# A graph network kernel on one core: VectorE's messages of the closing item, and TensorE's sums of them, stand one slot earlier in the step

## The chip, the cores and the metric

The kernel runs on one core of a Trainium2 chip. Times are microseconds on the device, from the start to the end of the program. The metric is the median over several executions. One further execution was recorded by the profiler, and all rows below come from it.

## The reference, cut to what matters

A graph has 6,250 nodes and 206,250 edges, sorted by destination. Three attention layers run over it, then a dense block with batch normalization. The change touches only the layers:

```python
xl = (x @ Wl + bl).reshape(n, heads, outc)
e_feat = leaky_relu(xl[src] + (x @ Wr + br).reshape(n, heads, outc)[dst], 0.2)
logits = einsum('ehc,hc->eh', e_feat, att)
m = segment_max(logits, dst)
a = exp(logits - m[dst])
a = a / segment_sum(a, dst)[dst]
out = segment_sum(xl[src] * a[:, :, None], dst)
```

`xl[src] * a` is what the kernel calls the messages, 128 numbers for each edge, and the outer `segment_sum` is what it calls the sums. Layer 1 also adds up 96 edge attributes for each node.

## The kernel before, in words

Edges are cut into chunks of 26 tiles of 128 edges. A chunk, together with a window of 128 destination nodes, is an *item*; each layer has 62 of them here. The 26 tiles of an item fall into 7 groups (`GROUPS`, `NG` = 7): six of four tiles and a last one of two.

All engines run the same software pipeline (`pipeline`), written out by hand in each engine's program. One *step* works on two items at once. It **opens** item k+1: its `xl` rows are gathered by GpSimd, TensorE expands the destination's transform (`expand`, line 763), VectorE adds the two into `z` (line 1186), takes the leaky ReLU with the attention vector (`am`, line 1193), adds up the heads (line 1202, in the last layer 1205) and adds the linear part (line 1216). In the same step it **closes** item k: VectorE finds the segment maxima by scans (lines 1243 to 1275), ScalarE takes the exponential (line 953), VectorE makes the messages (`message(g)`, line 1285), and TensorE sums them into one PSUM bank (`sums(g)`, line 791: 26 products, each of which stands as two passes in the trace, so 52 passes a step). When the last product is done, VectorE merges the item into the state of its nodes, beginning with `new_max` (line 1294), and only behind that does it come to the first group of the next step.

A step of each engine has 7 *slots*, g = 0 to 6. In slot g VectorE handles group g of the opening item. Which messages of the closing item it makes at the end of a slot is read from the table `SUMS_AT`, and TensorE reads its sums from the same table with one slot of delay:

```python
# VectorE, at the end of slot g
if closes and g == NG - 1: new_max()
if closes:
    for m in SUMS_AT.get(g, ()): message(m)
# TensorE, slot g
if opens and g + 2 < NG: expand(opens, g + 2)
if closes and stage == 0 and g in EA_CUTS: attribute_sums(EA_CUTS[g])
if closes:
    for m in SUMS_AT.get(g - 1, ()): sums(m)
```

`attribute_sums` (line 783) exists in layer 1 alone, in TensorE's slots 3, 4 and 5. GpSimd issues 26 gathers an item (line 706). Ahead of the gathers of group g it waits for `message(g)` of the item two before, whose buffer they fill, and for `z` of the group two before: so the gathers of the next item's group 0 wait for `z` of group 5, those of its group 1 wait for `z` of group 6, and those of its group 2 wait for the next step's first `z`. ScalarE makes the one-hot matrices `S` and `ST` for TensorE. SyncE loads the items; in layer 1 the loads of the edge attributes follow `attribute_sums`.

Of the kernel before, what the change touches and what calls it, by code (L numbers as in the profile page):

```python
# [46 lines left out]
NO_NODE = 100000  # L47
GROUPS = [range(a, min(a + 4, TILES)) for a in range(0, TILES, 4)]
NG = len(GROUPS)
SUMS_AT = {2: (0,), 3: (1, 2), 4: (3, 4), 5: (5, 6)}  # L50
EA_CUTS = {3: range(0, 9), 4: range(9, 18), 5: range(18, TILES)}
LH = TILES * HEADS
SQ = 32
# [49 lines left out]
def gnn_program(nc, x, x_t, edges_t, dst_rows, dst, dst_short, edge_attr, node_id, Wl, bl, Wr, br, att, c, g, be,  # L103
                u, W1, b1, gamma, beta, W2, b2, out):
    ctx = ExitStack()
    with ctx:
# [604 lines left out]
        def _(pe):  # L711
# [24 lines left out]
            for stage in range(LAYERS):  # L736

                def pe_step(opens, closes, begins, turned):
# [47 lines left out]
                    def sums(g):  # L786
                        q, v, use = closes
                        pe.wait_ge(onehot_done[g], v * 2)
                        pe.wait_ge(msg_done[g], v + 2)
                        for t in GROUPS[g]:  # L790
                            last = pe.matmul(agg_ps, S[:, q, t, :], msg[:, t, :], start=t == 0 and stage > 0, stop=t == TILES - 1)  # L791
                        if g == NG - 1:
                            last.then_inc(agg_done, 1)
# [3 lines left out]
                    for g in range(NG):  # L797
# [10 lines left out]
                        if closes:  # L808
                            for m in SUMS_AT.get(g - 1, ()):
                                sums(m)  # L810
# [230 lines left out]
        def _(dve):  # L1041
# [130 lines left out]
            def edge_step(stage, opens, closes, begins, turned):  # L1172
# [107 lines left out]
                def message(g):  # L1280
                    q, v, use = closes
                    a, n = GROUPS[g][0], len(GROUPS[g])
                    if g == 0:
                        dve.wait_ge(alpha_done, v)
                    dve.tensor_tensor(out=msg[:, a:a + n, 0:F].rearrange("p t (h f) -> p t h f", h=HEADS),  # L1285
                                      in0=xl_g[:, q, a:a + n, 0:F].rearrange("p t (h f) -> p t h f", h=HEADS),
                                      in1=msg[:, a:a + n, M_ALPHA:M_ONE].unsqueeze(3).to_broadcast([P, n, HEADS, F // HEADS]),
                                      op=ALU.mult).then_inc(msg_done[g], 1)
# [74 lines left out]
                for g in range(NG):  # L1363
# [24 lines left out]
                    if closes:  # L1388
                        for m in SUMS_AT.get(g, ()):
                            message(m)  # L1390
# [152 lines left out]
```

## Time and profile before

| | |
|---|---|
| median of 3 runs | 8529.99 us (8517.47 to 8535.05) |
| profiled execution, own time | 8491.84 us |
| its span on the core | 8489.9 us |
| mean granted TensorE clock | 0.679 |
| busy: TensorE, VectorE, ScalarE, GpSimd | 57%, 62%, 51%, 56% |

No engine is busy for much over half of the span, so the time is made of waits between engines, and one has to read steps, not shares. In a timeline row the columns are start, length, engine, line, operation, tiles and count; what stands in brackets is how long the engine sat idle before the row, and what ended that. "DVE" is VectorE, "PE" TensorE, "POOL" GpSimd. "issue" and "remote" mean that no other instruction of the profile explains the end of the idle time.

### The profile page before, as it was taken

What the parts mean: (1) busy time and instruction counts of PE and PEld (TensorE: products, weight loads), DVE (VectorE), ACT (ScalarE), POOL (GpSimd) and SP (SyncE); (2) the same over time, 40 slices, a digit from 0 to 9 for tenths busy, and PEclk for the clock granted to TensorE, in tenths of its full rate; (3) what the DMA queues carried; (4) which work ended last, traced back from release to release, by engine and by line L of the source; (5) the groups of instructions that cost most, each with busy time, mean ns of one, the idle gap of its engine ahead of it and who ended that gap; (6) DMA issues with size and microseconds to landing.
All of it is one profiled execution on the core that took longest, in us unless ns stands there. A gap on an engine that the chain in (4) does not pass through costs nothing.

```text
span 8489.9 us, 109176 instructions
## 1 busy us (share of the span) xinstructions
PE 4879.8 (57%) x24176; PEld 4286.7 (50%) x24176; DVE 5222.4 (62%) x16308; ACT 4307.0 (51%) x10681; POOL 4740.8 (56%) x4843
## 2 busy tenths in 40 slices
PE   4666666666666655555555555545555555544446
PEld 3565656565656544444444444444444444444444
DVE  5555565656565656766666667655555555555556
ACT  3444444444454545555555555545555555555546
POOL 3555555555555545666666666656666666666640
PEclk7666666666666666766767767666666666666666
DMA  5333333333333322322322323222222222222221
GB/s 147 94 100 91 96 97 97 97 96 97 96 98 95 98 67 74 79 76 76 77 75 77 82 77 78 76 66 72 77 71 71 72 72 72 76 73 72 72 61 50
DMA packets 460163, 697.83 MB, mean 82 GB/s; under 512 B 140781, under 2 KB 330019, under 8 KB 460101
## 3 DMA queue, kind: packets, MB, share of 16 engines
q0 software_dynamic: 154752, 327.15, 16.9%
q1 hardware_dynamic: 305349, 370.00, 14.2%
q8 instruction: 21, 0.34, 0.0%
q14 instruction: 41, 0.34, 0.0%
HBM read 638.95 MB, written 57.76 MB: 82 GB/s over the span
## 4 chain that ended last, share of the span: by engine, by line
PE 33%; issue 27%; DVE 22%; another core or an unknown queue 7%; ACT 6%; POOL 3%; DMA 2%; SPq 0%; DVEq 0%; ACTq 0%; POOLq 0%
PE PS L791 14%; PE PS L763 10%; PE PS L783 6%; DVE z L1186 3%; POOL xl_g L706 3%; DVE am L1193 3%; DVE msg L1285 2%; ACT distT L931 2%; ACT ST L936 2%; DVE relu_logit L1202 1%; ACT dist L906 1%; PE PS L749 1%; DMA xl_g<-xl_tab,edges 1%; DVE relu_logit L1205 1%
## 5 line engine op out<-in xcount | busy, mean ns | idle before, releaser
L706 POOL DMA_INDIRECT xl_g<-xl_tab,edges x4836 | 4740.0, 980 | 3485.8 <-DVE z L1186 1689.1
L763 PE MATMUL PS<-xr_w,ST 128*128 128x132 f32 x9672 | 2054.2, 373 | 2160.7 <-issue 1278.8
L763 PEld LDWEIGHTS PS<-xr_w,ST 128*128 128x128 f32 x9672 | 1778.9, 269 | 2455.4 <-issue 1735.2
L791 PE MATMUL PS<-msg,S 128*128 128x137 f32 x9672 | 1829.7, 352 | 936.8 <-issue 648.7
L791 PEld LDWEIGHTS PS<-msg,S 128*128 128x128 f32 x9672 | 1710.6, 257 | 1017.6 <-issue 1012.0
L1186 DVE TENSOR_TENSOR z<-PS,xl_g 128x528 f32<-128x528 f32 x1302 | 856.6, 658 | 1428.1 <-DMA xl_g<-xl_tab,edges 823.2
L906 ACT ACTIVATE dist<-node_row,neg_dst 128x128 f32<-128x128 f32 x4836 | 1534.5, 386 | 0.0
L931 ACT ACTIVATE distT<-dst_all,neg_node 128x512 f32<-128x512 int16 x1302 | 884.0, 679 | 1029.7 <-DVE neg_dst L1179 725.5
L909 ACT ACTIVATE S<-dist 128x512 f32<-128x512 f32 x1302 | 780.4, 599 | 839.9 <-remote 625.2
L1193 DVE SCALAR_TENSOR_TENSOR am<-z,att_relu 128x512 f32<-128x512 f32 x1302 | 860.8, 661 | 115.0 <-remote 94.1
L936 ACT ACTIVATE ST<-distT 128x512 f32<-128x512 f32 x1302 | 780.0, 599 | 42.6 <-ACT distT L931 1.4
L1285 DVE TENSOR_TENSOR msg<-xl_g,msg 128x512 f32<-128x512 f32 x1302 | 792.8, 644 | 0.2 <-ACT msg L953 0.2
L783 PE MATMUL PS<-ea,S 128*128 128x96 f32 x3224 | 628.6, 366 | 194.3 <-issue 194.1
L783 PEld LDWEIGHTS PS<-ea,S 128*128 128x128 f32 x3224 | 593.1, 278 | 260.3 <-issue 260.0
L1202 DVE TENSOR_REDUCE relu_logit<-am 128x16 f32<-128x512 f32 x868 | 557.0, 642 | 30.6 <-DVE am L1193 11.1
L1294 DVE TENSOR_SCALAR some<-PS 128x1 f32<-128x1 f32 x186 | 29.5, 158 | 836.2 <-PE PS L791 578.2
L966 ACT ACTIVATE rescale<-dmax 128x8 f32<-128x8 f32 x186 | 38.8, 208 | 879.0 <-DVE dmax L1304 802.1
L953 ACT ACTIVATE msg<-shifted 128x104 f32<-128x104 f32 x186 | 56.7, 305 | 716.0 <-issue 522.7
L1205 DVE TENSOR_REDUCE relu_logit<-am 128x4 f32<-128x512 f32 x434 | 278.3, 641 | 22.7 <-DVE am L1193 11.9
L1216 DVE TENSOR_TENSOR logit<-relu_logit,z 128x16 f32<-128x16 f32 x1302 | 227.5, 175 | 93.0 <-remote 82.1
L1243 DVE TENSOR_TENSOR_SCAN run_up<-row_pen,PS 128x128 f32<-128x128 f32 x186 | 77.8, 418 | 175.0 <-PE PS L770 98.7
L894 ACT COPY t_lr<-PS 128x264 f32<-128x264 f32 x124 | 46.9, 378 | 246.1 <-PE PS L749 168.7
(220 smaller groups left out, 3691.4 us busy)
## 6 DMA issues: line engine op xcount, KB each, us to landing
dst_all<-dst_short SPq DMA_DIRECT2D x186, 832.0 KB
xl_g<-xl_tab,edges POOLq DMA_INDIRECT x4836
ea<-edge_attr SPq DMA_DIRECT2D x124, 432.0 KB
ea<-edge_attr SPq DMA_DIRECT2D x62, 384.0 KB
xr_w<-xr_tab SPq DMA_DIRECT2D x186, 66.0 KB
dst_r<-dst_rows SPq DMA_DIRECT2D x186, 64.0 KB
node_row<-node_id SPq DMA_DIRECT2D x186, 64.0 KB
state<-t_new SPq DMA_DIRECT2D x126, 68.0 KB
```

The lines of the kernel that those rows point to most:

```text
L706: pool.indirect_dma_start(xl_g[:, q, t, :], None, xl_tab[stage][:, :], bass.IndirectOffsetOnAxis(idx[:, q, t:t + 1], 0))\
L763: last = pe.matmul(zp[(q + g) % 3][:, n, :], ST[:, t, :], xr_w[:, q, :], start=True, stop=True)
L783: last = pe.matmul(ea_ps, S[:, q, t, :], ea[:, q, t, :], start=False, stop=False)
L791: last = pe.matmul(agg_ps, S[:, q, t, :], msg[:, t, :], start=t == 0 and stage > 0, stop=t == TILES - 1)
L906: last = act.activation(dist[:, (q + g) % 2, m, :], node_row[:, q, :], ACT.Abs, bias=neg_dst[:, q, t:t + 1])
L909: act.activation(S[:, q, GROUPS[g][0]:GROUPS[g][0] + n, :], dist[:, (q + g) % 2, 0:n, :], ACT.Relu, bias=1.0, scale=-1.0)\
L931: act.activation(distT[:, (q + g) % 2, 0:n], dst_all[:, q, GROUPS[g][0] * P:GROUPS[g][0] * P + n], ACT.Abs, bias=neg_node[:, q:q + 1]).the ...
L936: act.activation(ST[:, GROUPS[g][0]:GROUPS[g][-1] + 1, :].rearrange("p t n -> p (t n)"), distT[:, (q + g) % 2, 0:n], ACT.Relu, bias=1.0, s ...
L1186: dve.tensor_tensor(out=z[:, (q + g) % 2, 0:n, :], in0=zp[(q + g) % 3][:, 0:n, :], in1=xl_g[:, q, a:a + n, :], op=ALU.add).then_inc(z_done ...
L1193: dve.scalar_tensor_tensor(am[:, (q + g) % 2, 0:n, :], z[:, (q + g) % 2, 0:n, 0:F], 0.0, att_relu[:, stage, :].unsqueeze(1).to_broadcast([ ...
L1202: s = dve.reduce_sum(relu_logit[:, a * HEADS:(a + n) * HEADS], am[:, (q + g) % 2, 0:n, :].rearrange("p t (h f) -> p (t h) f", h=HEADS), ax ...
L1285: dve.tensor_tensor(out=msg[:, a:a + n, 0:F].rearrange("p t (h f) -> p t h f", h=HEADS), in0=xl_g[:, q, a:a + n, 0:F].rearrange("p t (h f) ...
```

## The change

One line, a table:

```diff
-SUMS_AT = {2: (0,), 3: (1, 2), 4: (3, 4), 5: (5, 6)}
+SUMS_AT = {2: (0, 1), 3: (2, 3, 4), 4: (5, 6)}
```

No instruction is added or removed. On VectorE, message 1 moves from slot 3 to slot 2, messages 3 and 4 from slot 4 to slot 3, and messages 5 and 6 from slot 5 to slot 4; messages 0 and 2 stay in their slots. On TensorE the sums of groups 1, 3, 4, 5 and 6 move by one slot as well, since it reads the same table.

VectorE, a step of layer 3, slots 2 and 3 (the row with `z` 128x528 opens a slot):

```order
 L1205 TENSOR_REDUCE relu_logit<-am 128x4
-L1285 TENSOR_TENSOR msg<-xl_g,msg 128x4x128
-L1186 TENSOR_TENSOR z<-PS,xl_g 128x528
-L1216 TENSOR_TENSOR logit<-relu_logit,z 128x4x4
-L1193 SCALAR_TENSOR_TENSOR am<-z,att_relu 128x512
-L1205 TENSOR_REDUCE relu_logit<-am 128x4
 L1285 TENSOR_TENSOR msg<-xl_g,msg 128x4x128 x2
+L1186 TENSOR_TENSOR z<-PS,xl_g 128x528
+L1216 TENSOR_TENSOR logit<-relu_logit,z 128x4x4
+L1193 SCALAR_TENSOR_TENSOR am<-z,att_relu 128x512
+L1205 TENSOR_REDUCE relu_logit<-am 128x4
+L1285 TENSOR_TENSOR msg<-xl_g,msg 128x4x128 x3
```

Two messages now stand ahead of the `z` of group 3 where one stood, and three behind it where two stood.

VectorE again, the same step, slots 4 to 6 (the `z` of 128x264 is the last group's, of two tiles):

```order
-L1285 TENSOR_TENSOR msg<-xl_g,msg 128x4x128 x2
-L1186 TENSOR_TENSOR z<-PS,xl_g 128x528
-L1216 TENSOR_TENSOR logit<-relu_logit,z 128x4x4
-L1193 SCALAR_TENSOR_TENSOR am<-z,att_relu 128x512
-L1205 TENSOR_REDUCE relu_logit<-am 128x4
 L1285 TENSOR_TENSOR msg<-xl_g,msg 128x4x128
 L1285 TENSOR_TENSOR msg<-xl_g,msg 128x2x128
+L1186 TENSOR_TENSOR z<-PS,xl_g 128x528
+L1216 TENSOR_TENSOR logit<-relu_logit,z 128x4x4
+L1193 SCALAR_TENSOR_TENSOR am<-z,att_relu 128x512
+L1205 TENSOR_REDUCE relu_logit<-am 128x4
 L1186 TENSOR_TENSOR z<-PS,xl_g 128x264
```

The last two messages (groups 5 and 6) are made ahead of the `z` of group 5 instead of behind it, so that all seven messages stand ahead of that `z`, where five did.

TensorE, a step of layer 2 (line 763 with x2 is the expansion of the opening item's last group; an x counts products here, so half of the passes in the trace):

```order
 L763 MATMUL PS<-xr_w,ST 128x132 x4
 L788 REGISTER_ALU
-L791 MATMUL PS<-msg,S 128x137 x4
-L763 MATMUL PS<-xr_w,ST 128x132 x2
-L791 MATMUL PS<-msg,S 128x137 x22
+L791 MATMUL PS<-msg,S 128x137 x8
+L763 MATMUL PS<-xr_w,ST 128x132 x2
+L791 MATMUL PS<-msg,S 128x137 x18
```

The four products of group 1 move ahead of the last expansion. The order of the others stays; they come earlier only if their messages do.

TensorE, a step of layer 1, where the attribute products (line 783) stand between:

```order
-L791 MATMUL PS<-msg,S 128x137 x4
-L763 MATMUL PS<-xr_w,ST 128x132 x2
-L783 MATMUL PS<-ea,S 128x96 x9
-L791 MATMUL PS<-msg,S 128x137 x8
+L791 MATMUL PS<-msg,S 128x137 x8
+L763 MATMUL PS<-xr_w,ST 128x132 x2
+L783 MATMUL PS<-ea,S 128x96 x9
+L791 MATMUL PS<-msg,S 128x137 x12
 L783 MATMUL PS<-ea,S 128x96 x8
-L791 MATMUL PS<-msg,S 128x137 x14
+L791 MATMUL PS<-msg,S 128x137 x6
```

Eight more products of messages stand ahead of the last eight attribute products, four of them already ahead of the last expansion.

## Rows read from the trace of the kernel before

**Rows 1.** The page's costliest groups: mean ns of one, then idle before it
```profile
L1186 DVE TENSOR_TENSOR z<-PS,xl_g 128x528 f32<-128x528 f32 x1302 | 856.6, 658 | 1428.1 <-DMA xl_g<-xl_tab,edges 823.2
L1285 DVE TENSOR_TENSOR msg<-xl_g,msg 128x512 f32<-128x512 f32 x1302 | 792.8, 644 | 0.2 <-ACT msg L953 0.2
```
**Rows 2.** Line 1294 by layers: windows 194:3040, 3165:5649, 5767:8235, first to last one
```profile
L1294 DVE TENSOR_SCALAR some<-PS 128x1 f32<-128x1 f32 x61 | 9.7, 158 | 531.2 <-PE PS L791 417.6 <-remote 113.6
L1294 DVE TENSOR_SCALAR some<-PS 128x1 f32<-128x1 f32 x61 | 9.7, 158 | 139.4 <-PE PS L791 68.2 <-remote 36.5 <-issue 34.6
L1294 DVE TENSOR_SCALAR some<-PS 128x1 f32<-128x1 f32 x61 | 9.7, 159 | 146.2 <-PE PS L791 72.9 <-issue 54.2 <-remote 19.1
```
**Rows 3.** Timeline of VectorE, a step of layer 3
```profile
7023.07 0.68 DVE L1285 TENSOR_TENSOR msg<-xl_g,msg 128x512 f32<-128x512 f32 x1
...
7025.74 1.28 DVE L1285 TENSOR_TENSOR msg<-xl_g,msg 128x512 f32<-128x512 f32 x2
...
7032.24 1.28 DVE L1285 TENSOR_TENSOR msg<-xl_g,msg 128x512 f32<-128x512 f32 x2
7034.06 0.71 DVE L1186 TENSOR_TENSOR z<-PS,xl_g 128x528 f32<-128x528 f32 x1 [0.55 <-DMA xl_g<-xl_tab,edges]
...
7036.13 1.02 DVE L1285 TENSOR_TENSOR msg<-xl_g,msg 128x512 f32<-128x512 f32 x2
7042.90 0.43 DVE L1186 TENSOR_TENSOR z<-PS,xl_g 128x264 f32<-128x264 f32 x1 [5.75 <-remote]
...
7046.17 0.16 DVE L1294 TENSOR_SCALAR some<-PS 128x1 f32<-128x1 f32 x1 [1.90 <-PE PS L791]
```
**Rows 4.** Timeline of TensorE, the same step; x counts passes
```profile
7027.06 2.03 PE L791 MATMUL PS<-msg,S 128*128 128x137 f32 x8
...
7029.63 2.04 PE L791 MATMUL PS<-msg,S 128*128 128x137 f32 x16
7033.06 1.57 PE L791 MATMUL PS<-msg,S 128*128 128x137 f32 x10 [1.38 <-DVE msg L1285]
7037.14 0.39 PE L791 MATMUL PS<-msg,S 128*128 128x137 f32 x1 [2.52 <-issue]
...
7042.77 3.36 PE L791 MATMUL PS<-msg,S 128*128 128x137 f32 x14 [1.01 <-issue]
```
**Rows 5.** Timeline of GpSimd, the same step
```profile
7039.52 0.95 POOL L706 DMA_INDIRECT xl_g<-xl_tab,edges  x1 [0.31 <-issue]
7044.14 0.94 POOL L706 DMA_INDIRECT xl_g<-xl_tab,edges  x1 [3.67 <-DVE z L1186]
```
**Rows 6.** Timeline of TensorE, a step of layer 2
```profile
4522.87 2.64 PE L791 MATMUL PS<-msg,S 128*128 128x137 f32 x16
4530.74 5.27 PE L791 MATMUL PS<-msg,S 128*128 128x137 f32 x28 [5.23 <-issue]
```
**Rows 7.** Timeline of VectorE and TensorE, a step of layer 1
```profile
1038.88 1.02 DVE L1285 TENSOR_TENSOR msg<-xl_g,msg 128x512 f32<-128x512 f32 x2
...
1046.12 3.63 PE L791 MATMUL PS<-msg,S 128*128 128x137 f32 x16
```
**Rows 8.** Timeline of VectorE: line 1294 of three steps running, layer 1
```profile
1004.03 0.16 DVE L1294 TENSOR_SCALAR some<-PS 128x1 f32<-128x1 f32 x1 [8.49 <-PE PS L791]
...
1054.86 0.16 DVE L1294 TENSOR_SCALAR some<-PS 128x1 f32<-128x1 f32 x1 [9.21 <-PE PS L791]
...
1101.94 0.16 DVE L1294 TENSOR_SCALAR some<-PS 128x1 f32<-128x1 f32 x1 [8.75 <-remote]
```
**Rows 9.** Timeline of GpSimd: next item's first gather in the same two steps
```profile
1036.94 0.94 POOL L706 DMA_INDIRECT xl_g<-xl_tab,edges  x1 [0.88 <-issue]
...
1090.32 0.94 POOL L706 DMA_INDIRECT xl_g<-xl_tab,edges  x1 [4.15 <-DVE z L1186]
```
**Rows 10.** Timeline of VectorE: line 1294 of the next two steps, layer 3
```profile
7082.25 0.16 DVE L1294 TENSOR_SCALAR some<-PS 128x1 f32<-128x1 f32 x1 [0.82 <-PE PS L791]
...
7126.97 0.16 DVE L1294 TENSOR_SCALAR some<-PS 128x1 f32<-128x1 f32 x1 [2.31 <-issue]
```

## The prediction

> **What bounds the kernel now.** I read the page first, then the groups of instructions by line in each of the three layers, then the timeline of single steps, engine by engine, since no engine is busy enough to be the bound by itself.
>
> The closing item sets the length of a step: VectorE stands before line 1294, the merge, until TensorE's last sum is there. In each layer the window runs from the first to the last of 61 such rows, so over 60 steps: 2846, 2484 and 2468 us, which is 47.4, 41.4 and 41.1 us a step. VectorE's idle time there is 531.2, 139.4 and 146.2 us over 61, or 8.71, 2.29 and 2.40 us a step [rows 2]. That is the most that TensorE could give back if nothing else came up: 2.29 and 2.40 us a step in layers 2 and 3. It is not the price of the messages: VectorE makes all of them without waiting (0.2 us of idle in 1302, 644 ns each [rows 1]).
>
> The timeline of a layer 3 step shows why TensorE is late [rows 3, 4]. It ends the sums of groups 1 and 2 at 7031.67, waits 1.38 us for message 3, runs 10 passes in 1.57 us (0.157 us each), and then *stands* from 7034.6 on: 4 single passes with gaps of up to 2.52 us, which nothing in the profile explains, until 7042.77. The other 14 passes then take 3.36 us, 0.24 each, and VectorE's merge follows at 7046.17 after an idle 1.90 us. VectorE stood in the same stretch: its last `z` comes 5.75 us late, although the gathers that it needs were long issued. Both go on some 2.5 us after GpSimd's last gather ended (7039.52 + 0.95 = 7040.47), when GpSimd itself had to wait [rows 5]. So there is a common stand of all engines late in a step, tied to a long unbroken run of gathers. In layer 2 it catches TensorE right behind group 2: 5.23 us idle for no dependence, then 28 passes in 5.27 us, 0.188 each [rows 6].
>
> **The change part by part.**
>
> *VectorE, slots 2 and 3.* The `z` of group 3 comes one message later, 0.64 us, that of group 4 two messages, 1.29 us. `z` sits idle for 1428.1 / 1302 = 1.10 us on average already, over half of it for gathers [rows 1], so I charge nothing for group 3 (GpSimd is two groups behind and busy) and about 0.2 us for group 4, which the next slot gives back, as it has the short pair of messages (1.02 us) in place of a long one (1.28) [rows 3]. Uncovered, it would cost 0.64 us in the `z` of group 5.
>
> *VectorE, slot 5.* The two messages leave it: 1.02 us less between the `z` of groups 5 and 6. In layer 3 that only lengthens the 5.75 us before group 6. No price.
>
> *TensorE, layers 2 and 3.* Products lose their wait for messages 3 and 4, which now end at 7033.52 (7032.24 + 1.28) and would end near 7028.3: slot 3's messages would begin at 7025.74 + 0.64 and be three, 1.9 us [rows 3]. The expansion of group 6 comes one group of products later, at most 2.03 us [rows 4], well before its `z`. In the step shown TensorE would run on at 7031.67 instead of 7033.06: 1.38 us more of running before the stand, at 0.157 us 9 passes more. Messages 5 and 6 are in time for that: their slot begins its messages at 7032.24, so they end near 7033.3. If the stand begins at the same time as now, 5 instead of 14 passes are left behind it, 9 x 0.24 = 2.1 us less, more than the 1.90 us that VectorE waits there. If it begins at the same instruction, nothing is won. These are the two bounds for layer 3: 0 and 2.40 us a step. I take the middle, 1.2 us, since the 10 passes that ran before the stand show that some instructions are at hand even after a wait. Over 62 steps: 75 us.
>
> In layer 2 the bounds are 0 and 2.29 us. The stand there began while TensorE was idle [rows 6], so less can be pulled ahead of it, and I take a quarter, 0.6 us: 35 us.
>
> *TensorE, layer 1.* The last messages are made at 1039.9, but TensorE comes to the sums of group 1 only at 1046.12, behind its attribute products [rows 7]. Its queue is the bound, the queue is as long as before, and only its order changes. Nothing. The attribute loads are released up to eight products later, with most of a step to spare.
>
> *Given back.* An early merge meets GpSimd's gathers, which do not end earlier. One pair of steps shows it: 36.1 us (7046.17 to 7082.25), then 44.7 us (to 7126.97), together 80.8, or 40.4 each, against 41.1 for the layer [rows 2, 3, 10]: of 5 us won in one step, most is lost in the next. I charge 20 us for it in all, small since the gain here is spread over all steps.
>
> Sum: 75 + 35 - 20 = 90 us off. The profiled execution took 8491.84 us, 0.45% under the median of the runs shown (8529.99) and 0.3% under the lowest. It would take about 8402; carried over to the median, 8530 - 90 = 8440.
>
> **A rule weighed.** The stands in [rows 4] and [rows 6] look like engines waiting for their own instructions. The Trainium skill ("Runtime: NRT & Kernel Launch", Instruction fetch mechanics) says that each engine's instruction memory is refilled in blocks of a fixed number of instructions while the one before is worked off, mostly hidden, and that a taken branch costs a fetch. By that rule a stand would sit at a place in the program, moved work could not slip ahead of it, and the sum would be nothing, the rival below. That fetching is what is late here no row can show.
>
> **The rivals.**
>
> *The stand is tied to the instruction.* For it: in layer 2 TensorE stands exactly at the first product of group 3 [rows 6]. Against it: in layer 3 it is 10 passes further. Then TensorE waits less for messages and more in the stand, and the merge comes when it did: 8530.
>
> *The full gain.* The stand is tied to time alone, and TensorE's queue is done when VectorE is: 2.2 us in layer 3 and 1.5 us in layer 2, 62 steps each, 230 us: 8300.
>
> *GpSimd pauses more often.* In layer 1 a step with 0.88 us of pause before the next item's first gather takes 50.83 us (1004.03 to 1054.86); the next one, with a pause of 4.15 us, takes 47.08, 3.75 less [rows 8, 9]. The pause ends the stand earlier. With two more instructions ahead of `z` of group 5, VectorE may be caught before it, and GpSimd must pause. If ten steps turn over, 40 us: 8490.
>
> *Slower: the gathers start later.* The same delay of group 5's `z`, in steps whose pause is long anyway, only moves the next item's gathers. In the row shown the `z` has just 0.55 us of slack before its gathers land [rows 3]. From the point where VectorE's stand begins ahead of that `z`, instead of behind it, a message's time (0.64 us) is lost in each step. If that holds for layers 1 and 2, 124 steps, it is 80 us: 8610; if for one of them, 8570.
>
> **How the numbers follow.** Forecast, part of TensorE's wait saved: 0.37. Full gain: 0.10. More pauses: 0.10. Tied to the instruction, no change: 0.15. Slower: 0.28. The range 8290 to 8580 takes in the first four but for half of the full gain's own spread, and the milder half of the slow case; the forecast's own range is 8350 to 8510. About 0.2% of the time, 17 us, is what a measurement can tell from no change. Faster by more: 0.37 + 0.10 + 0.10 = 0.57; within: 0.15; slower: 0.28.
>
> **What the profile after would show.** Line 791 no longer waits for line 1285. In layers 2 and 3 more passes of line 791 lie before the stand, and VectorE's idle before line 1294 falls from 2.29 and 2.40 us to some 1.7 and 1.2; in layer 1 it stays near 8.7. The steps shorten to about 40.8 and 39.9 us in layers 2 and 3. I would be wrong if TensorE stands from the same pass on, if the `z` of group 5 comes later, or if the time before the first `z` of a step grows by what line 1294 gains.

## The result, and the profile after

| | before | changed |
|---|---|---|
| median, same session | 8523.06 us (8509.83 to 8535.05, 10 runs) | 8544.67 us (8528.85 to 8560.01, 10 runs) |
| ratio | | 1.0027, 95% interval 1.0017 to 1.0037 |
| profiled execution, own time | 8491.84 us | 8559.77 us |
| its span | 8489.9 us | 8557.9 us |
| mean granted TensorE clock | 0.679 | 0.682 |

The changed kernel is 21.6 us slower. The two profiled executions lie 67.9 us apart, more than the medians: that of before is faster than all ten of its timed runs, that of the changed kernel is at the upper end of its own. One must keep that in mind in every comparison of the two traces.

The page of the changed kernel, costliest groups (mean ns of one, then idle time before it):

```profile
L706 POOL DMA_INDIRECT xl_g<-xl_tab,edges x4836 | 4698.0, 971 | 3595.5 <-DVE z L1186 1961.1
L791 PE MATMUL PS<-msg,S 128*128 128x137 f32 x9672 | 1863.6, 351 | 1007.9 <-issue 999.5
L1186 DVE TENSOR_TENSOR z<-PS,xl_g 128x528 f32<-128x528 f32 x1302 | 855.4, 657 | 1026.4 <-DMA xl_g<-xl_tab,edges 554.6
L1285 DVE TENSOR_TENSOR msg<-xl_g,msg 128x512 f32<-128x512 f32 x1302 | 778.5, 645 | 0.2 <-ACT msg L953 0.2
```

The same groups on the page of before:

```profile
L706 POOL DMA_INDIRECT xl_g<-xl_tab,edges x4836 | 4740.0, 980 | 3485.8 <-DVE z L1186 1689.1
L791 PE MATMUL PS<-msg,S 128*128 128x137 f32 x9672 | 1829.7, 352 | 936.8 <-issue 648.7
```

Three things moved. TensorE's idle time before the sums did not fall but rose by 71.1 us, and nearly all of it now ends without a dependence ("issue"). VectorE waits 401.7 us less before `z` [rows 1]. GpSimd waits 272.0 us longer for `z`.

Line 1294 by layers in the changed kernel: first the instructions with their first and last start, then the groups with the idle time before them (windows 197:3084, 3209:5723, 5843:8301).

```profile
L1294 DVE TENSOR_SCALAR some<-PS x61: 157/158/160, 197.9 to 3083.5; 128x1 f32<-128x1 f32 x61
L1294 DVE TENSOR_SCALAR some<-PS x61: 157/157/160, 3209.8 to 5722.2; 128x1 f32<-128x1 f32 x61
L1294 DVE TENSOR_SCALAR some<-PS x61: 157/157/160, 5843.6 to 8300.7; 128x1 f32<-128x1 f32 x61
...
L1294 DVE TENSOR_SCALAR some<-PS 128x1 f32<-128x1 f32 x61 | 9.7, 158 | 590.1 <-PE PS L791 335.8 <-remote 254.3
L1294 DVE TENSOR_SCALAR some<-PS 128x1 f32<-128x1 f32 x61 | 9.6, 158 | 88.0 <-PE PS L791 65.2 <-issue 22.7
L1294 DVE TENSOR_SCALAR some<-PS 128x1 f32<-128x1 f32 x61 | 9.6, 158 | 125.7 <-PE PS L791 90.5 <-issue 23.5 <-remote 11.8
```

Over 60 steps that is 48.1, 41.9 and 41.0 us a step, where [rows 2] gave 47.4, 41.4 and 41.1. VectorE's idle time before the merge went from 531.2, 139.4 and 146.2 us to 590.1, 88.0 and 125.7. In layer 2 it fell by 51.4 us over the layer while the layer grew by 28.7: the merge is not what a shorter wait there makes earlier. VectorE's idle time between the merge and the first `z` of a step, added up from the trace over the 60 steps, grew from 130.7 to 206.9 us in layer 2 and from 148.2 to 223.4 in layer 3.

### The profile page after: what moved, and what is told of

Same layout as the page of the kernel before. It is cut to its first block, busy times and chain, and to the rows that moved or that the text cites. A ratio compares the mean times of both kernels' runs of the same rounds, so it can differ in the third digit from the quotient of the medians.

```text
span 8557.9 us, 109176 instructions
## 1 busy us (share of the span) xinstructions
PE 4852.4 (57%) x24176; PEld 4257.0 (50%) x24176; DVE 5209.1 (61%) x16308; ACT 4307.3 (50%) x10681; POOL 4698.8 (55%) x4843
## 4 chain that ended last, share of the span: by engine, by line
PE 29%; DVE 27%; issue 27%; another core or an unknown queue 8%; ACT 4%; DMA 2%; POOL 1%; SPq 0%; DVEq 0%; ACTq 0%; POOLq 0%
PE PS L791 12%; PE PS L763 9%; DVE z L1186 4%; PE PS L783 4%; DVE msg L1285 4%; DVE am L1193 3%; DVE relu_logit L1202 2%; ACT distT L931 2%; ACT ST L936 1%; POOL xl_g L706 1%; DMA xl_g<-xl_tab,edges 1%; DVE t_newton L1342 1%; PE PS L749 1%; DVE t_rstd L1343 1%
## 5 line engine op out<-in xcount | busy, mean ns | idle before, releaser
L791 PE MATMUL PS<-msg,S 128*128 128x137 f32 x9672 | 1863.6, 351 | 1007.9 <-issue 999.5
L783 PEld LDWEIGHTS PS<-ea,S 128*128 128x128 f32 x3224 | 560.9, 270 | 42.4 <-issue 42.4
L783 PE MATMUL PS<-ea,S 128*128 128x96 f32 x3224 | 578.0, 356 | 4.7 <-issue 4.6
L885 ACT ACTIVATE t_hT<-PS,be_col,g_col 128x128 f32<-128x128 f32 x124 | 56.7, 457 | 290.0 <-PE PS L743 279.2
```

Source lines behind the costliest of these rows:

```text
L783: last = pe.matmul(ea_ps, S[:, q, t, :], ea[:, q, t, :], start=False, stop=False)
```

## What the sessions showed first: two levels of the same kernel

The experiments ran in five further sessions. In three of them the kernel before takes 7189.81 to 7192.80 us, in two 8516.47 and 8538.63 us. The records number the chip 13 in two sessions of the first kind and in one of the second (4 and 14 in the others), so it is not the chip by itself (the expectations below still say "chip", where it is the session). All ratios below are against the kernel before in the same session. I call the levels **7190** and **8520**.

The kernel before, profiled in a session of level 7190 (its copy has one more line at the top, so each line number is one higher), costliest groups:

```profile
L707 POOL DMA_INDIRECT xl_g<-xl_tab,edges x4836 | 4751.9, 983 | 2173.3 <-issue 1581.0
L792 PE MATMUL PS<-msg,S 128*128 128x137 f32 x9672 | 1510.9, 315 | 457.5 <-DVE msg L1286 457.5
L1286 DVE TENSOR_TENSOR msg<-xl_g,msg 128x512 f32<-128x512 f32 x1302 | 792.2, 644 | 0.2 <-ACT msg L954 0.2
```

A gather and a message take as long as before (983 against 980 ns, 644 against 644). What is gone is above all idle time: GpSimd waits 1312.5 us less, and the span is 1302.5 us shorter (7187.4 against 8489.9). TensorE's idle time before the sums is a wait for messages and nothing else. Its passes are shorter as well, 315 against 352 ns at a granted clock of 0.723 against 0.679, and its busy time is 514.9 us less (4364.9 against 4879.8); how much of the 1302.5 us that is worth was not separated. The common stand of all engines, which the prediction read in [rows 3, 4, 6], does not exist at this level. The levels lie 7 us a step apart, some sixty times the 21.6 us / 186 that the change costs. What makes the stand come and go between sessions no row shows.

What the engines wait for in it can be read in part. A step of the kernel before in layer 1, level 8520, whose merge is the last row of [rows 8]:

```profile
1096.32 3.48 PE L791 MATMUL PS<-msg,S 128*128 128x137 f32 x28
1099.27 0.94 POOL L706 DMA_INDIRECT xl_g<-xl_tab,edges  x1 [0.30 <-issue]
```

TensorE's last sum, the only thing that the merge waits for, ends at 1099.80, and the merge starts at 1101.94, 1.73 us after GpSimd's last gather of the run has ended. The semaphore came late. The trace has a time for many semaphore updates, which can be set beside the end of the last instruction that makes them. In the kernel before at level 8520, 1489 of the 16105 updates matched in this way come over 1 us after it; at level 7190 (26842 matched) a single one does. In the other profiles of level 8520 it is 1374 to 1963 updates, in the others of level 7190 none. The late ones belong to TensorE, VectorE and ScalarE; of GpSimd's own 1124 one is late. So at level 8520 engines stand in part because updates reach them late, and 1047 of the 1489 arrive while GpSimd pauses for over 0.6 us between gathers. In layer 2 such updates crowd in two places of a step, some 30 to 38 and some 6 to 10 us after the merge: there is a second, smaller stand, ahead of the step's first `z`. TensorE also pauses between passes of one group, where it waits for no semaphore, so late updates are not all of it, and what holds them back stays open. The trace has also only 17668 update records of these semaphores here, against 33707 of the same program at level 7190; whether the recording has a part in the stand no run shows.

## The experiments

Most split the one table into two, so that VectorE and TensorE can be moved apart:

```diff
-SUMS_AT = {2: (0,), 3: (1, 2), 4: (3, 4), 5: (5, 6)}
+MSGS_AT = {2: (0,), 3: (1, 2), 4: (3, 4), 5: (5, 6)}
+SUMS_AT = {2: (0,), 3: (1, 2), 4: (3, 4), 5: (5, 6)}
...
-                        for m in SUMS_AT.get(g, ()):
+                        for m in MSGS_AT.get(g, ()):
                             message(m)
```

### The parts of the change, level 7190

Messages alone:

```diff
-MSGS_AT = {2: (0,), 3: (1, 2), 4: (3, 4), 5: (5, 6)}
+MSGS_AT = {2: (0, 1), 3: (2, 3, 4), 4: (5, 6)}
```

> VectorE's messages in the new slots, TensorE's sums in the old ones. Theory A (the loss comes from VectorE: the common stand of all engines now catches it in slot 4, ahead of the z of group 5, so that z and GpSimd's next gathers come later): the whole loss is here, some 15 to 30 us over before (8523), like after (8545). Theory B (the loss comes from TensorE's order, the last expansion behind the sums of group 1): no loss here, 8515 to 8530.

Sums alone:

```diff
-SUMS_AT = {2: (0,), 3: (1, 2), 4: (3, 4), 5: (5, 6)}
+SUMS_AT = {2: (0, 1), 3: (2, 3, 4), 4: (5, 6)}
```

> TensorE's sums in the new slots, VectorE's messages in the old ones, so TensorE waits for messages 1, 3, 4, 5 and 6 where it stands, message 1 ahead of the last expansion. Theory A: within 10 us of before. Theory B: 20 us or more over before.

Only messages 5 and 6:

```diff
-MSGS_AT = {2: (0,), 3: (1, 2), 4: (3, 4), 5: (5, 6)}
+MSGS_AT = {2: (0,), 3: (1, 2), 4: (3, 4, 5, 6)}
```

> Only messages 5 and 6 move, from behind the z of group 5 to the end of slot 4, four messages in a row there; TensorE as before. Theory A in its narrow form (the two extra messages directly ahead of that z make it late): z of group 5 up to 1 us later, a loss of 20 us or more. If it is instead the messages ahead of slot 4's flags that push these into the stand, this one loses little: within 10 us of before.

Only messages 1, 3 and 4:

```diff
-MSGS_AT = {2: (0,), 3: (1, 2), 4: (3, 4), 5: (5, 6)}
+MSGS_AT = {2: (0, 1), 3: (2, 3, 4), 5: (5, 6)}
```

> Messages 1, 3 and 4 in the new slots, 5 and 6 in the old slot 5, TensorE as before. Counterpart of the one before it: the narrow theory expects no loss, 8515 to 8530; the theory of the flags pushed into the stand expects the whole of it, 8540 or more.

Measured: messages alone 7103.23 us, 0.9881 (0.9866 to 0.9896); sums alone 7193.79, 1.0004 (0.9995 to 1.0014); messages 5 and 6 alone 7128.27, 0.9914 (0.9901 to 0.9928); messages 1, 3 and 4 alone 7256.47, 1.0091 (1.0075 to 1.0106). The theories of these four expectations speak of the stand, which isn't there at this level, so they are not tested here. The messages are the whole change at this level. Messages 5 and 6 alone give 62.0 of the 87.0 us: TensorE's queue ends with their sums. The earlier three by themselves cost 66.2 us, 0.9%, but added to 5 and 6 they give the other 25.0. By themselves they only lengthen TensorE's idle time between the sums of group 4 and the late ones of 5: 487.8 us against 457.5 over the kernel, and the passes are slower, 325 ns against 315. The rows for TensorE in two windows in layers 2 and 3 (busy, passes, granted clock, share of DMA, GB/s), first with messages 1, 3 and 4 moved:

```profile
2700.00:4700.00 2000.00, 1183.62 (x6030) 0.69 0.34 87
4900.00:6800.00 1900.00, 1054.68 (x5838) 0.69 0.34 87
```

and in the kernel before:

```profile
2700.00:4700.00 2000.00, 1167.56 (x6196) 0.73 0.35 90
4900.00:6800.00 1900.00, 1038.99 (x5919) 0.74 0.34 87
```

The granted clock, a mean between the levels of 1.2 and 2.4 GHz, is 0.69 instead of 0.73 in the kernel with the longer idle time. A later `z` is not what costs: in layer 2 the `z` of group 3 starts 0.5 us later after the merge, those of groups 4 and 5 no later (25.4 and 30.6 us, against 25.5 and 30.7; means of 60 steps). Of TensorE's time, 30.3 us more are idle before the sums and 47.7 us more are busy in them (1558.5 against 1510.9).

### Before and changed kernel side by side

The two kernels unchanged, and the messages alone again:

> The kernel before, unchanged, profiled beside the changed one on the same chip. The kernel before took 8523 us on one chip and 7190 us on another. Theory A (the difference between chips is the common stand of all engines late in a step, some 5 us in each of 186 steps): if it takes about 8520 here, the last expansion and z of group 5 show idle time put down to nothing in the profile (issue, remote: over 2000 us of TensorE's idle in all), and GpSimd's idle before its gathers is about 3500 us; if about 7190, these idle times are gone, GpSimd's idle is about 2200 us, and mean durations of all instructions are those of the slower chip within 1%. Theory B (the chips differ in TensorE's clock): the durations of TensorE's passes differ by far more than 1% and the idle time does not.

> The changed kernel, unchanged, beside the one before. Theory A (the sign hangs on the stand: where it is there, what VectorE has ahead of z of group 5 falls into it and the next item's gathers go out later; where it is absent, the earlier messages only give TensorE its work sooner, as with the messages alone at 0.9881): ratio 0.986 to 0.990 on a chip that takes 7190 us for the kernel before, 1.002 to 1.004 on one that takes 8520. Theory B (the earlier sums undo what the earlier messages give, whatever the chip): 0.998 to 1.004 on either chip.

> VectorE's messages in their new slots, TensorE's sums in their old ones. Theory A: 0.987 to 0.989 on a chip that takes 7190 us for the kernel before; on one that takes 8520, 1.000 to 1.005, since z of group 5 still comes late. Theory B (the sums' place is what costs): 0.985 to 0.990 on either chip, and the changed kernel beside it is slower by over 0.8%.

The session was of level 7190. The changed kernel took 7105.74 us against 7189.81, **0.9885 (0.9869 to 0.9901)**; the messages alone 7103.62, 0.9882 (0.9866 to 0.9897). So the same edit is 1.15% faster at one level and 0.27% slower at the other. Theory A of the expectation for the changed kernel holds (no stand, no loss), and its rival, the earlier sums undoing the gain, is out. Of the expectation for the kernel before neither theory holds whole: the idle times went as A has them, but TensorE's passes differ by 10%, not by under 1%. The clock alone can't be it, since VectorE's waits for its own small instructions are gone as well: before line 1343 (1344 in the copy), which reads what VectorE itself has just made, it was idle for 22.4 us in layer 2 at level 8520, and for 6.2 us here.

The kernel before at level 7190, by layers (windows 176:2532, 2643:4781, 4883:6931); the first three rows give first and last start, then come the idle times of layers 2 and 3:

```profile
L1295 DVE TENSOR_SCALAR some<-PS x61: 157/158/159, 176.6 to 2531.5; 128x1 f32<-128x1 f32 x61
L1295 DVE TENSOR_SCALAR some<-PS x61: 157/158/160, 2644.0 to 4780.1; 128x1 f32<-128x1 f32 x61
L1295 DVE TENSOR_SCALAR some<-PS x61: 141/158/160, 4883.8 to 6930.3; 128x1 f32<-128x1 f32 x61
...
L792 PE MATMUL PS<-msg,S 128*128 128x137 f32 x3125 | 506.0, 321 | 239.9 <-DVE msg L1286 239.9
L1295 DVE TENSOR_SCALAR some<-PS 128x1 f32<-128x1 f32 x61 | 9.6, 158 | 31.0 <-PE PS L792 29.2
...
L792 PE MATMUL PS<-msg,S 128*128 128x137 f32 x3127 | 527.4, 331 | 204.2 <-DVE msg L1286 204.2
```

The changed kernel beside it (windows 176:2532, 2640:4707, 4810:6846), the same rows:

```profile
L1295 DVE TENSOR_SCALAR some<-PS x61: 157/158/159, 176.6 to 2531.3; 128x1 f32<-128x1 f32 x61
L1295 DVE TENSOR_SCALAR some<-PS x61: 141/148/150, 2640.6 to 4706.1; 128x1 f32<-128x1 f32 x61
L1295 DVE TENSOR_SCALAR some<-PS x61: 141/147/151, 4810.0 to 6845.5; 128x1 f32<-128x1 f32 x61
...
L792 PE MATMUL PS<-msg,S 128*128 128x137 f32 x3120 | 469.6, 312 | 31.3 <-DVE msg L1286 31.1
L1295 DVE TENSOR_SCALAR some<-PS 128x1 f32<-128x1 f32 x61 | 9.0, 148 | 0.0
...
L792 PE MATMUL PS<-msg,S 128*128 128x137 f32 x3120 | 480.8, 317 | 60.2 <-DVE msg L1286 59.8
```

Per step: layer 1 2354.9 / 60 = 39.2 us in both, layer 2 35.6 to 34.4, layer 3 34.1 to 33.9. TensorE's wait for messages in layer 2 falls from 239.9 to 31.3 us, VectorE's wait for TensorE from 31.0 to 0, and the layer is 70.6 us shorter. In layer 3 the merge's wait falls as much, from 33.1 us to 0, but VectorE then waits for TensorE in another place, line 1244, ahead of the step's first `z`; kernel before, then changed:

```profile
L1244 DVE TENSOR_TENSOR_SCAN run_up<-row_pen,PS 128x128 f32<-128x128 f32 x60 | 25.3, 421 | 97.2 <-PE PS L771 97.2
L1244 DVE TENSOR_TENSOR_SCAN run_up<-row_pen,PS 128x128 f32<-128x128 f32 x60 | 25.2, 421 | 173.9 <-PE PS L771 165.1 <-issue 8.8
```

76.7 us more are lost there, which is why this layer becomes only 11.0 us shorter.

### A delay that was none

Twelve sequencer increments ahead of `z` of group 5, in the kernel before:

```diff
                         for m in MSGS_AT.get(g, ()):
                             message(m)
+                    if closes and g == 4:
+                        for _ in range(12):
+                            dve.sem_inc(spacer, 1)
```

> The kernel before with 12 more sequencer increments of a semaphore on VectorE at the end of slot 4, behind messages 3 and 4 and ahead of z of group 5, so that this z and all behind it come later by the time they take (some 0.06 us each, 0.7 us in all). Theory A (the next item's gathers are what the step ends on, and z of group 5 sends them): slower by 0.5 to 1.5% on a chip of 8520 us, and by half of that or less on one of 7190 us where VectorE's idle before z takes it up. Theory B (z of group 5 has slack): within 0.2% on both.

Measured: 7192.84 us, 1.0004 (0.9994 to 1.0013). This looks like theory B, but the trace gives `z` of group 5 at the same place as without them (30.7 us after the merge in layer 2, mean of 60 steps, in both). The increments, some 0.09 us apart in the trace, were worked off while VectorE was busy with messages, so the run says nothing on the price. The next ones use real work.

### A stand put in by hand, level 8520

Seven sums over heads whose result nobody uses, in slot 4 behind the flags (ahead of messages 5 and 6 in the changed kernel, and of `z` of group 5 in both), or the same in slot 5, behind that slot's `sum_heads` and ahead of its messages:

```diff
                         if g == 4:
                             flags()
+                            q, v, use = opens
+                            dve.wait_ge(logit_done[g], v * 3 - 2)
+                            for k in range(7):
+                                dve.reduce_sum(scratch[:, k, :], am[:, (q + g) % 2, 0:4, :].rearrange("p t (h f) -> p (t h) f", h=HEADS), axis=AX.X)
```

> The kernel before, with a stand put in by hand: 7 more sums over heads (128x512, 0.64 us each, 4.5 us, results used by nobody) on VectorE in every slot 5, behind its own sum over heads and ahead of messages 5 and 6, which is where VectorE stood in the kernel before on the first chip. Numbers for a chip that takes 7190 us without it. Theory A (the price of a stand is what TensorE and VectorE have left to do behind it): messages 5 and 6 come 4.5 us later, layers 2 and 3 take 4.5 us a step more and layer 1, whose TensorE comes to those sums only at 37.6 us, 1.4 more: about 7835. Theory B (what counts is z of group 5, which is not moved here): much less, 7190 to 7400.

> The changed kernel with the same 7 sums behind the flags of slot 4, ahead of messages 5 and 6 and of z of group 5, where VectorE stood in the changed kernel on the first chip. Theory A: VectorE's own row of work sets the step in layers 2 and 3 (plus 4.5 us) and nearly so in layer 1 (plus 0.5): about 7105 + (0.5 + 4.5 + 4.5) x 62 = 7690, which is 1.8% under the same stand in the kernel before. Then VectorE's stand alone does not turn the sign, and what turned it on the first chip lies with TensorE or GpSimd. Theory B (VectorE's stand falling ahead of z of group 5 delays the next item's gathers, and that is the loss): 7835 or more, at or over the kernel before with its stand.

> The kernel before with the same 7 sums behind the flags of slot 4: z of group 5 and messages 3 to 6 all come 4.5 us later. Beside the same stand in slot 5 it tells what the later z of group 5, and so the later gathers, cost by themselves. Theory A: within 0.5% of it. Theory B: slower than it by 2% or more.

> The changed kernel with the same 7 sums in slot 5, behind z of group 5 and behind all seven messages. Theory A: VectorE's row of work is as long as with them behind the flags of slot 4, so within 0.5% of that, about 7690. Theory B: faster than that by 2% or more, since z of group 5 is not late.

The session was of level 8520, with the real stand beside the one made by hand, so the sums of the expectations don't apply, but the comparisons do:

| | slot 5, behind `z` of group 5 | slot 4, ahead of it |
|---|---|---|
| kernel before | 8704.26 us, 1.0226 (1.0209 to 1.0244) | 8813.85 us, 1.0351 (1.0334 to 1.0369) |
| changed kernel | 8547.23 us, 1.0031 (1.0019 to 1.0044) | 8844.12 us, 1.0392 (1.0372 to 1.0412) |

Two groups of the changed kernel with the work behind `z` of group 5 (two lines more at the top):

```profile
L1392 DVE TENSOR_REDUCE scratch<-am 128x16 f32<-128x512 f32 x1302 | 789.4, 677 | 13.8 <-DVE relu_logit L1207 6.3
...
L793 PE MATMUL PS<-msg,S 128*128 128x137 f32 x9672 | 1817.2, 348 | 952.5 <-issue 944.8
```

789.4 us of work were added to VectorE, 4.24 us a step, and the kernel is where the changed kernel was without them (1.0031 against 1.0027, inside both intervals). VectorE has that much room behind its last message; even the `z` of group 6, which stands behind the added work, costs nothing by coming later (in layer 1 at 40.9 us after the merge, against 37.0). The same work in slot 4, in the same kernel, costs 8844.12 - 8547.23 = 296.9 us, 1.60 us a step, or 0.38 us for each us of delay; in the kernel before, where messages 5 and 6 come later either way, 109.6 us, 0.14 for each. These are prices of `z` of group 5 together with the messages that stand behind the added work in slot 4 alone (5 and 6 in the changed kernel, 3 and 4 in the kernel before), so for `z` by itself they are upper bounds. They are not even over the layers: by the profiled executions, slot 4 costs the changed kernel 2.6, 2.7 and -0.4 us a step in layers 1, 2 and 3, and the kernel before 2.9, 0.1 and -0.9. Theory B (it is `z` of group 5) foresaw the signs; of its two margins of 2% or more, one came (3.4%) and the other not (1.3%). Theory A (within 0.5% of each other) had neither. In the kernel before the work in slot 5 costs 187.8 us, 0.24 for each us; in the changed kernel, where messages 5 and 6 stand ahead of it, nothing, so it is these two that cost.

In layer 1 the way of the loss shows. With the work in slot 4 TensorE's last sum ends no later than with it in slot 5 (45.4 against 46.1 us after the merge in the changed kernel, 45.7 against 46.0 in the kernel before), but the next merge follows 4.7 and 4.2 us behind it, instead of 1.4 and 1.1: it waits for nothing but the late semaphore.

### The parts of the change, level 8520

The same four kernels as at level 7190:

> VectorE's messages 1, 3 and 4 one slot earlier, 5 and 6 left behind z of group 5, TensorE's sums in their old slots. Numbers for a chip that takes about 8520 us for the kernel before. Theory B (messages 5 and 6 ahead of z of group 5 are the loss; the earlier 3 and 4 give a little of the forecast's gain): faster than before, 0.990 to 0.998. Theory C (messages 1, 3 and 4, which make z of groups 3 and 4 later, are the loss): 1.002 to 1.006. On a chip of about 7190 us: 1.009, as before.

> Only messages 5 and 6 one slot earlier, TensorE's sums in their old slots. On a chip of 8520 us, theory B: slower, 1.003 to 1.010. Theory C: 0.995 to 1.001. On a chip of 7190 us: 0.991, as before.

> All messages in their new slots, TensorE's sums in their old ones. On a chip of 8520 us, theories B and C: 1.002 to 1.004, as the changed kernel. Theory D (on this kind of chip the order of the sums is the loss, since TensorE stands right behind the sums that it now runs ahead of its last expansion, which z of group 6 needs): 0.990 to 0.998. On a chip of 7190 us: 0.988, as before.

> TensorE's sums in their new slots, messages in their old ones. On a chip of 8520 us, theories B and C: 0.999 to 1.001. Theory D: 1.002 to 1.008. On a chip of 7190 us: 1.000, as before.

| | level 7190 | level 8520 |
|---|---|---|
| messages 1, 3, 4 alone | 1.0091 | 8564.87 us, 1.0029 (1.0018 to 1.0040) |
| messages 5, 6 alone | 0.9914 | 8582.12 us, 1.0051 (1.0038 to 1.0064) |
| all messages | 0.9881 | 8584.87 us, 1.0048 (1.0035 to 1.0061) |
| sums alone | 1.0004 | 8537.43 us, 0.9997 (0.9988 to 1.0006) |
| all (the change) | 0.9885 | 1.0027 (1.0017 to 1.0037) |

Theory D, the order of the sums, is out. Of B and C neither holds alone: either part of the messages loses, and the two don't add up. Messages 5 and 6 turn from most of the gain into the larger loss, 43.5 us; by the prices above, 1.02 us of messages ahead of `z` of group 5 in 186 steps should cost 27 to 72 us. That the two figures agree does not show that this `z` is the cause: against the sums alone, profiled in the same session, messages 5 and 6 make it 0.2 us later in layer 1 and 0.6 in layer 2. Why messages 1, 3 and 4 lose 0.29% was not tested; they stand ahead of the `z` of groups 3 and 4. That the sums give back some of the loss of the messages (1.0048 to 1.0027) rests on two sessions and on intervals that overlap.

### A new profile of before, and z first

```diff
-MSGS_AT = {2: (0,), 3: (1, 2), 4: (3, 4), 5: (5, 6)}
+MSGS_AT = {2: (0,), 3: (1, 2), 5: (3, 4, 5, 6)}
```

> The kernel before, unchanged, profiled again; numbers for a session in which it takes about 8520 us. Theory B as first put (the change moves VectorE's stand ahead of z of group 5): line 1186's z of group 5 starts 31.6 to 32.1 us after the merge in layers 1 and 2, as in the first profile. Theory E (the stand lies at VectorE's flags of slot 4 in either kernel, and the first profile, at 8492 us the fastest execution of 20, was unusual): it starts at 34 to 36 us, as with the sums alone, and the page's idle time before message exponentials (line 953) is near 900 us instead of 716. If the session is of the 7190 us kind: 31.4 and 30.7 us, as before.

> Messages 3 to 6 all behind z of group 5, sums in their old slots: the table for messages is 2: 0; 3: 1, 2; 5: 3, 4, 5, 6. In a session of 8520 us, theory B (the step hangs on z of group 5 and not on the messages): 0.990 to 0.998. Theory F (both count about alike, as the two partial changes of 1.003 and 1.005 suggest; messages 3 and 4 come some 5 us later): 1.003 to 1.015. In a session of 7190 us: 1.005 to 1.02, since there TensorE waits for messages.

The session was of level 7190, so the first run (7182.76 us) has no stand to show, and its question was not answered. Messages 3 to 6 behind `z` of group 5 took 7623.12 us, 1.0598 (1.0584 to 1.0613), far over the 1.005 to 1.02 expected: TensorE waits 724.2 us for messages, against 457.5. Early messages are worth much where nothing stands. At level 8520 this kernel wasn't tried, so theories B and F of its expectation, and theory E of the other, stand untested.

## Why the prediction was wrong

**The step that failed** is "TensorE, layers 2 and 3": that TensorE, with its messages in time, would run more passes ahead of the stand and end sooner. It does the first and not the second. Timeline of the changed kernel, a layer 2 step at level 8520 (merge at 4296.22, the next at 4337.58, 41.36 us), VectorE, then TensorE:

```profile
4322.38 1.89 DVE L1285 TENSOR_TENSOR msg<-xl_g,msg 128x512 f32<-128x512 f32 x3
...
4328.22 0.18 DVE L1228 TENSOR_TENSOR tile_eq<-ends_T 128x25 f32<-128x25 f32 x1 [1.15 <-DVE ends_T L1226]
4331.02 0.28 DVE L1235 TENSOR_TENSOR through<-tile_eq,tile_one 128x26 f32<-128x26 f32 x2 [2.39 <-issue]
...
4332.74 0.70 DVE L1186 TENSOR_TENSOR z<-PS,xl_g 128x528 f32<-128x528 f32 x1
...
4337.58 0.16 DVE L1294 TENSOR_SCALAR some<-PS 128x1 f32<-128x1 f32 x1 [1.40 <-PE PS L791]
...
4326.18 1.10 PE L791 MATMUL PS<-msg,S 128*128 128x137 f32 x8
4329.61 0.39 PE L791 MATMUL PS<-msg,S 128*128 128x137 f32 x1 [2.33 <-issue]
4331.71 0.39 PE L791 MATMUL PS<-msg,S 128*128 128x137 f32 x1 [1.71 <-issue]
4332.43 5.12 PE L791 MATMUL PS<-msg,S 128*128 128x137 f32 x26 [0.33 <-issue]
```

The kernel with the sums alone moved, whose VectorE runs the program of before, a step of the same length in the same layer (merge at 4268.35, the next at 4309.70, 41.35 us):

```profile
4302.20 0.28 DVE L1236 TENSOR_TENSOR through<-tile_eq,tile_one 128x26 f32<-128x26 f32 x2 [1.73 <-remote]
...
4302.99 1.28 DVE L1286 TENSOR_TENSOR msg<-xl_g,msg 128x512 f32<-128x512 f32 x2
4304.19 0.70 DVE L1187 TENSOR_TENSOR z<-PS,xl_g 128x528 f32<-128x528 f32 x1
...
4309.70 0.16 DVE L1295 TENSOR_SCALAR some<-PS 128x1 f32<-128x1 f32 x1 [1.15 <-issue]
...
4298.49 1.10 PE L792 MATMUL PS<-msg,S 128*128 128x137 f32 x8
4304.48 5.18 PE L792 MATMUL PS<-msg,S 128*128 128x137 f32 x28 [4.88 <-DVE msg L1286]
```

Messages 3 and 4 are ready 28.0 us after the merge in the one (4324.27) and 35.9 us after it in the other (4304.27), 7.9 us apart. TensorE has nothing in its way in the one and waits 4.88 us in the other. Yet it runs two single passes inside the stand and 26 behind it, where the other runs 28 behind it, in 5.12 and 5.18 us, and the merges come 41.36 and 41.35 us after the last. Freed of its wait, TensorE stood in the same stretch: two passes are what 7.9 us of earlier messages gave. The prediction had reckoned with 9 passes in layer 3. The means of 60 steps say the same: in layer 2 messages 3 and 4 are ready 28.2 against 34.5 us after the merge, and TensorE's last sum ends at 41.8 us in both; in layer 3 it ends at 40.8 against 41.0. That the gain comes where the stand is absent (0.9885 at level 7190) shows the same from the other side.

Point by point:

- *VectorE, slots 2 and 3: no charge for `z` of group 3, 0.2 us for that of group 4.* Right at level 7190, where only the `z` of group 3 comes later, and the 0.91% that messages 1, 3 and 4 cost by themselves is TensorE's time. At level 8520 they cost 0.29% by themselves (26.2 us), but next to nothing once 5 and 6 are moved as well (8582.12 to 8584.87 us); whether through `z` was not tested.
- *TensorE, layer 1: nothing.* Right at level 7190: 39.2 us a step before and after. At level 8520 47.4 became 48.1, and 47.7 with the sums alone. TensorE's queue ends as early as there (46.7 against 46.8 us after the merge), as predicted; what is longer is the wait of the merge for the late semaphore, 1.4 us behind TensorE's last sum instead of 0.8 (0.04 at level 7190). In the 34 steps of the changed kernel where it is over 0.5 us, the merge comes 1.98 us after the end of GpSimd's last gather, in 80% of them within 1.90 to 2.00. Against the sums alone the changed kernel takes 0.4 us a step more in layer 1, 25 us in all, and within 0.1 us the same in layers 2 and 3; all messages alone, profiled in the same session as the sums alone, take 0.5, 0.25 and 0.1 us more. So most of the loss lies in layer 1, where the prediction put nothing, as far as single profiles can show it.
- *TensorE, layer 2: 0.6 us a step; layer 3: 1.2 us.* At level 7190 layer 2 gave 1.18 us and layer 3 0.2 us (70.6 and 11.0 us over 60 steps), the two terms nearly the other way round; layer 3 loses most of its gain to the wait at line 1244. Their sum with what is given back, 90 us, is close to the 84.07 us measured. That is luck in part: it was worked out for a stand that this level doesn't have. (62 steps of 0.6 us are 37 us, not 35.)
- *The stand is tied to the instruction* (the rival of no change, and the rule of the Trainium skill, "Runtime: NRT & Kernel Launch", Instruction fetch mechanics, that was weighed with it). TensorE's end did not move, and it stands from the first pass of group 3 on, as in [rows 6]: both as this rival said. But the stretch ends 36.2 us after the merge in the one step above (4332.43) and 36.1 us in the other (4304.48), with two passes worked off inside it and none, so it ends at no fixed instruction. (This is weak: in the second step TensorE's own end of the stand can't be seen, since it waits for messages made at 4304.27, and VectorE's stand ends ahead of the same line, 1235, in both steps, 34.8 and 33.9 us after the merge. In [rows 3] it ends ahead of the last `z`.) That fetching is what stands no row shows, and two things speak against it: the trace has 62 packets of kind "instruction" in the whole span of the kernel before, at either level, and none at all between 600 and 3000 us, while some 50 steps of layer 1 stand there; and a refill that is mostly hidden, as the rule has it, would be so at both levels. The Trainium skill also has a taken branch cost a fetch only where its target lies outside the instructions that are held, which the prediction left out.
- *Slower: the gathers start later.* The direction came true, but that this is the cause is not shown. Against the sums alone, `z` of group 5 starts 0.1 us later in layer 1, 1.0 us later in layer 2 (36.6 against 35.6) and 0.4 us earlier in layer 3, and it is layer 1 that became longer. Work put in by hand says that a late `z` can cost, at most 0.14 to 0.38 us for each us over the three layers and at most 0.7 in the worst of them, so the prediction, which took the whole delay of 0.64 us as lost, priced it too high.
- *GpSimd pauses more often.* Also seen in the pair of profiles: in layer 2 the steps with a short pause (2.8 us or less) ahead of the next item's first gather are 3 of 59 instead of 13. But the kernel with the sums alone has 0 of 59 and is no faster than before, so this is no cause.
- *The signs of being wrong.* All three were seen: TensorE stands from the same pass on in layer 2; `z` of group 5 comes later (32.1 to 36.6 us in layer 2, of which 3.5 also come with the sums alone); and the time before the first `z` of a step grows by what the merge's wait gains, in layer 2 by 76.2 us against 51.4. That last one is the second stand.

**A second error lay under it.** The prediction took the profile of before as typical of where the stand falls on VectorE. VectorE's idle time before two lines of the flags, layer 1, kernel before (window 194:3040):

```profile
L1235 DVE TENSOR_TENSOR through<-tile_eq,tile_one 128x26 f32<-128x26 f32 x120 | 17.4, 187 | 52.2 <-remote 27.4 <-DVE tile_one L1229 15.5 <-issue 9.2
L1226 DVE STREAM_TRANSPOSE ends_T<-ends 128x64 f32<-128x64 f32 x60 | 14.7, 245 | 5.8 <-DVE ends L1224 2.1 <-issue 1.6
```

Changed kernel (197:3084):

```profile
L1235 DVE TENSOR_TENSOR through<-tile_eq,tile_one 128x26 f32<-128x26 f32 x120 | 16.9, 183 | 96.6 <-remote 70.1 <-issue 24.3 <-DVE tile_one L1229 2.0
L1226 DVE STREAM_TRANSPOSE ends_T<-ends 128x64 f32<-128x64 f32 x60 | 14.7, 246 | 88.5 <-remote 38.3 <-DVE ends L1224 35.8 <-issue 14.1
```

Sums alone (194:3056):

```profile
L1236 DVE TENSOR_TENSOR through<-tile_eq,tile_one 128x26 f32<-128x26 f32 x120 | 17.0, 184 | 101.9 <-remote 87.3 <-issue 8.3 <-DVE tile_one L1230 6.4
L1227 DVE STREAM_TRANSPOSE ends_T<-ends 128x64 f32<-128x64 f32 x60 | 14.7, 245 | 24.4 <-DVE ends L1225 12.7 <-issue 7.2 <-remote 3.4
```

58.0 us before, 185.1 changed, and 126.3 where VectorE's program is that of before. More than half of what looks like the work of the change comes without any message moved, in a kernel that is no slower than the one before (0.9997). `z` of group 5 in layer 1 starts 31.6, 34.3 and 34.2 us after the merge in the three (means over 60 steps). In the profiles of all three kernels with messages moved in part or in whole at this level (1, 3, 4; 5, 6; all) it starts at 34.1 us or later too. Whoever compares the two profiles alone finds a `z` 2.7 us later and a neat cause. That the first profile was an untypical execution is likely by this, and not shown.

What stays open: what holds the semaphore updates back, what decides the level, by what way the messages cost their 0.3 to 0.5% where the stand is, and whether a new profile of before at level 8520 would look like that of the sums alone.

## What to carry to other kernels

An idle time that nothing explains is not room that earlier work can fill: find out first whether it stays when its neighbour moves, and give "the wait is replaced by the stand" the chance that the forecast gets. Where two profiled executions are further apart than the medians, compare with a third kernel that has one half of the change before telling a story. Look in the trace whether a semaphore came when its instruction ended: where it came late, earlier work on the engine that sends it may give nothing. And where one operation releases another engine's transfers, price it by putting real work ahead of it and behind it, and see what else the work delays; twelve semaphore increments on the sequencer delayed nothing here.

## What was not expected of the hardware

The same program takes 7190 us in some sessions and 8520 in others, 18.5% more, at granted clocks of 0.723 and 0.68, with equal durations of gathers and messages; the chip's number is 13 at both levels. The sign of a 1% change hangs on it: 0.9885 there, 1.0027 here. Where the program is slow, about one in eleven of the matched semaphore updates comes over 1 us after its instruction (1489 of 16105), where it is fast none but one of 26842. And 789.4 us of added work on VectorE cost nothing that could be measured at level 8520, placed behind the last message and `z` of group 5.
